# First normalisation in pairs of tiles, and the expert weights spread over 128 rows

## What is computed

```python
x = x + tanh(g_xattn[0]) * L0_attention(layernorm(x), ctx, ctx)      # 32 heads, 8 key heads
x = x + tanh(g_ffn[0])   * L0_ffn(layernorm(x))                      # quantised weights, hidden 704
x = x + tanh(g_xattn[1]) * L1_attention(layernorm(x), ctx, ctx)      # 16 heads, 4 key heads, projection
x = x + tanh(g_ffn[1])   * L1_moe(layernorm(x))                      # 32 experts, top 8 per token
...
h = silu(einsum('th,eih->tei', x, w_gate)) * einsum('th,eih->tei', x, w_up)
h = h * masked_w[:, :, None]          # softmax over the 8 chosen router logits, zero elsewhere
out = einsum('tei,ehi->th', h, w_down)
```

## Time and profile before

| what | before |
|---|---|
| median of 3 runs | 442.41 us |
| the profiled execution | 442.06 us |
| its span, first to last instruction | 440.3 us |
| mean granted TensorE clock | 0.984 of 2.4 GHz |
| busy: PE / DVE / ACT / POOL | 391.7 / 301.8 / 223.9 / 216.4 us |
| chain that ended last | PE 51% of the span, DVE 3%, ACT 1%, issue 1% |

### The profile page before, as it was taken

How to read it: one execution, slowest core, us unless ns; L and a number is a source line. 1 busy time by engine, 2 the same in 40 slices (tenths; PEclk the granted TensorE clock), 3 DMA queues, 4 the chain that set the end, 5 groups by cost and what they waited for, 6 DMA issues and landing times.

```text
span 440.3 us, 6773 instructions
## 1 busy us (share of the span) xinstructions
PE 391.7 (89%) x2248; PEld 333.2 (76%) x2248; DVE 301.8 (69%) x603; ACT 223.9 (51%) x446; POOL 216.4 (49%) x234
## 2 busy tenths in 40 slices
PE   0697879897987988979999999999999999999994
PEld 0486778797986987957788887887687777788773
DVE  5486768878766877657678776665867665666664
ACT  2586766575556653535565544444454444444431
POOL 6788976643166533236666253544343344443510
PEclk9998989999999999969999999999999999999999
DMA  5921111000000000031321212223232343333101
GB/s 162 206 71 39 36 37 37 0 2 2 0 1 1 1 2 0 7 102 38 106 63 47 71 44 66 74 71 96 69 88 77 102 122 107 83 97 89 57 0 48
DMA packets 14339, 25.58 MB, mean 58 GB/s; under 512 B 4513, under 2 KB 7201, under 8 KB 14305
## 3 DMA queue, kind: packets, MB, share of 16 engines
q1 hardware_dynamic: 14304, 25.15, 20.1%
HBM read 24.10 MB, written 1.05 MB: 57 GB/s over the span
## 4 chain that ended last, share of the span: by engine, by line
PE 51%; DVE 3%; ACT 1%; issue 1%; DVEq 0%; ACTq 0%
PE bank L1250 15%; PE bank L1252 14%; PE bank L1251 14%; PE bank L1337 2%; PE bank L1149 1%; PE bank L1130 1%; PE bank L1172 1%; PE bank L1110 1%; DVE h_t L980 1%; PE bank L1205 1%; PE bank L1327 0%; ACT ot L623 0%; DVE hl L985 0%; DVE t_t L974 0%; DVE t_t L961 0%
## 5 line engine op out<-in xcount | busy, mean ns | idle before, releaser
L523 POOL TENSOR_TENSOR wl<-wraw,wh 128x768 fp32r<-128x768 f32 x48 | 88.7, 1848 | 109.3 <-DVE hl L985 109.3
L1250 PE MATMUL bank<-xh,wh 128*128 128x512 f32 (+1 forms) x288 | 109.2, 379 | 3.5 <-DVE t_t L961 3.5
L1252 PE MATMUL bank<-xh,wl 128*128 128x512 f32 (+1 forms) x288 | 103.3, 359 | 0.0
L1251 PE MATMUL bank<-xl,wh 128*128 128x512 f32 (+1 forms) x288 | 103.1, 358 | 0.0
L623 ACT ACTIVATE hh<-h_t 128x512 fp32r<-128x512 f32 (+1 forms) x72 | 40.3, 559 | 100.3 <-DVE h_t L980 83.0
L985 DVE TENSOR_TENSOR hl<-h_t,hh 128x512 fp32r<-128x512 f32 (+1 forms) x72 | 49.1, 682 | 24.8 <-ACT hh L623 24.7
L1250 PEld LDWEIGHTS bank<-xh,wh 128*128 128x128 f32 x288 | 55.2, 192 | 11.6 <-issue 3.2
L1252 PEld LDWEIGHTS bank<-xh,wl 128*128 128x128 f32 x288 | 55.0, 191 | 8.1
L961 DVE SCALAR_TENSOR_TENSOR t_t<-s_t,bank 128x512 f32<-128x512 f32 (+1 forms) x72 | 42.9, 595 | 26.3 <-ACT s_t L768 25.9
L1250 PE MATMUL bank<-hh,wh 128*128 128x512 f32 (+1 forms) x144 | 53.2, 370 | 8.4 <-DVE x L996 5.6
L1251 PEld LDWEIGHTS bank<-xl,wh 128*128 128x128 f32 x288 | 55.3, 192 | 7.0
(11 more groups left out here) (105 smaller groups left out, 616.0 us busy)
## 6 DMA issues: line engine op xcount, KB each, us to landing
wraw<-w SPq DMA_DIRECT2D x54, 384.0 KB, 3.1
out<-x SPq DMA_DIRECT2D x8, 128.0 KB, 2.4
x<-x_in SPq DMA_DIRECT2D x1, 768.0 KB, 5.0
ctx_v<-ctx_in SPq DMA_DIRECT2D x2, 256.0 KB, 7.0
ctx_k<-ctx_t SPq DMA_DIRECT2D x2, 192.0 KB, 3.3
x<-x_in SPq DMA_DIRECT2D x1, 256.0 KB, 2.7
wc<-wc_t SPq DMA_DIRECT2D x1, 256.0 KB, 3.9
ot<-sel_in SPq DMA_DIRECT2D x1, 256.0 KB, 5.3
```

Of the source, the lines that this page charges most:

```text
L523: ops.tensor_tensor(wl[:, slot, :], src, wh[:, slot, :].bitcast(F32), ALU.subtract).then_inc(F.w_split, 1)
L1250: nc.tensor.matmul(o, wh[:, slot, w_sl], rh, start=first, stop=False, skip_group_check=reopened)
L1251: nc.tensor.matmul(o, wh[:, slot, w_sl], rl, start=False, stop=False, skip_group_check=reopened)
L1252: return nc.tensor.matmul(o, wl[:, slot, w_sl], rh, start=False, stop=stop, skip_group_check=reopened)
```

## The change

For layer 0, statistics and powers of tiles 2 to 7 are taken two at a time: at ticks 1, 9 and 17, for tiles t + 2 and t + 3; ticks 5, 13 and 21 have none. The spread product takes all 128 rows: `sel` and `wts` grow to 128 partitions, rows 64 to 127 of both are zero. For `sel` the zeros come with a load of twice the size; for `wts` POOL clears the whole tile once, in step 4, and ACT's first writer of `wts` waits for that.

```diff
-        sel_raw = ot[0:2 * EXPERTS].rearrange("p k n -> p (k n)")
-        sel = sb("sel", [2 * EXPERTS, QUADS * P], F32R)
-        wts = sb("wts", [2 * EXPERTS, 2, BLK], F32R)
+        sel_raw = ot[:].rearrange("p k n -> p (k n)")
+        sel = sb("sel", [P, QUADS * P], F32R)
+        wts = sb("wts", [P, 2, BLK], F32R)
...
+                if u == 1 and t % 2 == 0 and t + 2 < TT:
+                    power(a, t + 2, t + 4)
                 if u == 1 and t + 2 < TT:
-                    power(a, t + 2, t + 3)
                     if n == 9:
                         pool.wait_ge(kl_ready, 3)
                     key_part(a, t + 2, 1)
...
+                if s == 4:
+                    ops.memset(wts[:].bitcast(F32), 0.0).then_inc(R.wt_zero, 1)
...
             def route_high(h):
                 act.wait_ge(R.wt_done, h + 1)
+                act.wait_ge(R.wt_zero, 1)
                 copy(wts[0:EXPERTS, h, :], bank[PB][0:EXPERTS, :]).then_inc(R.wt_hi, 1)
...
-                if u == 1 and t + 2 < TT:
+                if u == 1 and t % 2 == 0 and t + 2 < TT:
                     if t == 0:
                         dve.wait_ge(x_loaded[1], 16)
-                    ln_stats(a, t + 2, t + 3)
+                    ln_stats(a, t + 2, t + 4)
...
-        "sel_in": np.tile(np.repeat(np.eye(EXPERTS, dtype=np.float32), 32, axis=1), (2, 1)),
+        "sel_in": np.pad(np.tile(np.repeat(np.eye(EXPERTS, dtype=np.float32), 32, axis=1), (2, 1)),
+                         ((0, P - 2 * EXPERTS), (0, 0))),
```

More of the change, by code:

```diff
@@ L290, in __init__ @@
         self.wt_lo = sem("r_wt_lo")
+        self.wt_zero = sem("r_wt_zero")
         self.sel_loaded = sem("r_sel_loaded")
```

## The result

The changed kernel took 437.42 us (median of 4 runs, 437.04 to 438.23) against 442.26 us before: a ratio of 0.9888 (changed over before), with a 95% interval of 0.9863 to 0.9913. It is faster, by 4.8 us, where 9 us were forecast, and 0.4 us above the forecast range. The profiled execution took 437.19 us, its span 435.4 us, at a mean granted clock of 0.974 (before 0.984). POOL, DVE, ACT and PE are busy for 215.2, 300.6, 224.0 and 388.4 us.

A forecast was written before the change was run, and what follows sets the result against it. PE was taken to bound the experts' half, POOL to be busiest in the attention alone. 6.24 + 1.20 - 0.49 + 1.20 + 1.00 = 9.15 us off 442.06 us, plus 0.35 us to the median: 433.3 us, range 430.0 to 437.0 us.

The forecast's parts named there:

- the sum's last one: Whole kernel: all terms together take 9.15 us off the profiled execution of 442.06 us, giving 432.9 us.
- the early part: Attention-only stretch, 11 to 56 us: pairing statistics and powers of layer 0 gives 2.91 us.
- The sign that the prediction named: Granted clock at 0.50 in new places would put the sum off by 0.20 us for each product there.
- The slower rival: Moved waits bring the 1.2 GHz clock to busy PE stretches; 46 more slow products use up 9.15 us; chance 0.04.
- The spread: 16 spread products in the experts' half: 128 rows remove a gap of 0.39 us each, 6.24 us in all.
- PE finishes one shape before it starts another: At the spread product: its 64-row shape causes the 0.39 us delay, on the way in and out.
- Powers at ticks 5 and 13: POOL in the attention: removing one tile's power brings the chain to PE's wait 1.20 us earlier at each tick.
- pairs: Two-tile powers at ticks 1, 9 and 17: nothing lost at 1 and 17, a cost of 0.49 us at 9.
- tick 21: Power removed there: POOL's key product and DVE's subtraction end 1.20 us earlier; 1.0 us taken as gain.
- The additions: Clearing `wts` (some 0.90 us, in POOL's idle time) and doubling the `sel` load to 512 KB: no cost.
- Spread only: Rival: another wait replaces POOL's in the attention, so the early part gives nothing; 436.2 us, chance 0.17.
- The gap is not the shape: Rival: operand change or semaphore wait causes the spread's gap, so only the early part is left; 439.5 us, chance 0.12.

The follow-up runs named there:

- the spread alone: The changed kernel with layer 0's statistics and powers put back to one tile at a time: 437.62 us, ratio 0.9861 against the kernel before.
- the pairs alone: The kernel before with only the paired statistics and powers, its spread product keeping 64 rows: 441.4 us, ratio 0.9951.

## Why the prediction was wrong

**The step that failed** is the sum's last one, "9.15 us off the profiled execution": it took the falls of the clock from the one profile of before, with a single late fall, as part of the program. They are not: three profiles of the changed kernel have three different sets of falls. In the first, two more late falls, of 2.33 and 2.57 us, took back the lead of the early part, and the measured difference is 4.8 us instead of 9. Part of that is the luck of the draw: the first measurement set four slow executions of the changed kernel beside four fast ones of the kernel before, and the two later ones, 435.3 and 436.43 us, lie within the forecast range. At equal falls the three profiles give 8.3 to 8.6 us, so the sum's terms together are 0.6 to 0.9 us too high, and the rest of the miss is the clock. The sign that the prediction named, 0.50 in new places, is what came (0.50 at 176 to 180 us). The slower rival spoke of the clock, but tied it to waits that the change moves, where the spread alone, which moves none by more than 0.22 us up to the first of them, had new falls too; with its condition wrong, its small form (a fall or two more, 2.4 us each, 435.7 to 438.1 us) was in no case and the range ended at 437.0 us. The 0.9 us that a measurement was said to tell from no change came from three runs within 0.3 us; the later executions of the kernel before lie between 441.7 and 446.6 us.

**The spread** was right in that the 64 rows make the gap, and nearly right in size: 0.37 us a time instead of 0.39, the gap gone on both sides. Behind 208 us, 15 of the 16 are 5.55 us, of which 4.95 came: 0.28 stayed at the second routing, where PE's wait for DVE grew from 1.02 to 1.30 us, and 0.23 at the transposes at 231 us (1.08 us behind the product ahead of them, 0.85 before). That PE finishes one shape before it starts another does not hold as put: 96 rows among 128 bring no gap. The drain estimated from the Trainium skill's page TensorE: Matmul & The Clock Gate (Step-by-step: what each phase is for), 0.107 us, would have been too small beside the 0.37 us.

**Powers at ticks 5 and 13, pairs, tick 21.** The mechanism was right, and the sizes a little low. Counted from PE's first transposes, which came 0.13 us later than before (10.98 and 10.85), PE is 1.30 us ahead at tick 7 (1.20 forecast), 0.84 at tick 11 (0.71), 2.37 at the wait at 68 us (1.91), and 3.69 at the wait at 83 us and at 99.71 us (2.91). The two profiles do not have the same falls in this stretch either (before at 40 and 60 us, changed at 48), so the excess need not be the pairs'. PE's wait at tick 15 is gone altogether, and its wait at tick 7 is 0.87 us. At tick 21 DVE's subtraction took 1.18 us instead of the 2.10 in the earlier trace rows, still ending behind POOL's key product (78.35 to 80.25); the next one, at 84.38 with POOL idle, took 0.42 us:

```profile
79.36 1.18 DVE L990 TENSOR_TENSOR hl<-h_t,hh 128x256 fp32r<-128x256 f32 x1 [0.49 <-ACT hh L627]
```

The one wait forecast to grow, by 0.5 us at tick 11, grew by 1.75, from 1.25 to 3.00 us, and one not forecast to grow, at 68 us, from 0.73 to 1.86; yet both end as early as the sum has them, or earlier. The lead of 3.56 us was given back to the falls and not to another wait.

**The additions** cost nothing that shows: the clearing of `wts` lies in POOL's idle time with 3.05 us left behind it, and the larger load of `sel` landed in 4.3 us.

**The rivals.** "Spread only" gives 436.2 us, close to the time measured, and for a wrong reason: the pairs alone measured 2.2 us by themselves. "The gap is not the shape" is refuted by the spread alone, as far as 64 rows go.

**What stays open:** what decides whether a fall follows a wait, and whether the change makes falls more frequent: over all executions the difference is 7.5 us, about 1 us less than at equal falls.

## What to carry to other kernels

Before a sum is made against one profiled execution, look where its granted clock falls and ask whether the other executions have the same falls; price each long wait of TensorE with a chance of one, and compare kernels over many executions, or place by place between profiles. Here a product with half the rows, between products of full rows, cost 0.37 us more than its place, and padding it with zeros to the neighbours' rows cost nothing that shows. Where a busy engine off the main path fed a wait of the main one, taking 1.20 us of small instructions out of it paid in full, since the wait was longer than that.

## What the runs showed of the hardware that I had not expected

The same program has its clock fall behind different waits of PE in different executions: of waits of 1.9 to 3.0 us at about 49, 100, 134, 173 and 191 us some are followed by a fall and some are not. Over the twelve profiles a fall came behind the wait at 100 us in 6 of 11, at 134 in 5 of 8, at 173 in 5 of 9 where it was 2.0 us, and at the first routing in 9 of 11. A wait of 1.30 us was followed by one, too, in 2 of 3. And a product of 96 rows between products of 128 runs at their pace, with no gap, while one of 64 rows costs 0.37 us more.
